# Gathered expert rows on GpSimd: two fetches and two additions per solver period, in front of the first subtraction, instead of one of each behind it

## The chip, the core and the metric

The kernel is one program on one core of a Trainium2 chip. Its five engines run their own instruction streams and meet through semaphores: TensorE (PE) multiplies, VectorE (DVE), ScalarE (ACT) and GpSimd (POOL) work on tiles, and SyncE (SP) issues most of the transfers. The metric is the device time of one execution in microseconds (us).

## The reference, cut to what matters

The reference runs two layers. The first is a delta-rule attention over 8 sequences of 256 tokens with 16 heads of 128, and a mixture of eight experts of which each token gets two. Both add into the same residual rows, so their order is free:

```python
def step(state, inp):
    qt, kt, vt, bt = inp
    pred = jnp.einsum('bhd,bhdv->bhv', kt, state)
    delta = bt[..., None] * (vt - pred)
    state = state + jnp.einsum('bhd,bhv->bhdv', kt, delta)
    ot = jnp.einsum('bhd,bhdv->bhv', qt, state)
    return (state, ot)
...
def expert_body(acc, ws):
    gw, uw, dw, cwe = ws
    y = _mlp(x2d, gw, uw, dw)
    return (acc + cwe[:, None] * y, None)
routed, _ = jax.lax.scan(expert_body, jnp.zeros_like(x2d), (gate_w, up_w, down_w, cw.T))
out = routed.reshape(orig_shape) + _mlp(x, shared_gate_w, shared_up_w, shared_down_w)
```

The second layer is an attention that learns its weights as it goes, and six experts of which each sequence gets two.

## The kernel before

All 2048 tokens stay on the chip, as `X`: 16 tiles (`NT`) of 128 rows by 256 columns. The experts of the first layer run first. They read rows sorted by expert, and write their weighted results, in the same sorted order, to `slot_out` in the chip's memory. Each token has two rows there (`TOP0` is 2), so 32 pieces have to be brought back, one for each of its two experts and each of the 16 tiles. Numbered by `i`, from 0 to 31, a piece is handled in two steps on POOL:

- `fetch(i)` (line 2346) issues one indirect DMA that gathers 128 rows of `slot_out` into buffer `i % GBUF` of `gathered`. From the `GBUF`-th on it first waits until the addition that used the buffer is done.
- `add_fetched(i)` (line 2353) waits for the landing and adds the buffer into a tile of `X`.

Before the first fetch POOL waits until SP's stores of `slot_out` are done (`e_stored`).

The attention of the first layer is a pipeline of 64 units: 16 heads by 4 blocks (`NBLK`) of 512 tokens. `period(h, j)` exists once for each engine, with an order written out by hand, and works on up to five units at a time: `u0` is the newest, `u3` the one whose result is added to `X`. The solver for a unit inverts a triangular matrix in levels and corrects the solution twice. What the engines hand each other near the edited place is this:

- ACT copies the first solution of a unit to `Wu` when PE has made it (`keep_first`, line 1369). POOL's period ends inside the next period of ACT, so the unit is `u1` for POOL and `u2` for ACT here.
- POOL then makes `Rm`, right side minus `Wu` (`rhs_minus(u1, 0, 0)`, lines 2387 to 2393). DVE adds a product of PE to `Rm` and gets `Rb` (`residual`, line 1885), from which PE works out the correction (line 760), which DVE applies (`refine`, line 1891).
- POOL starts the next period with `add_squares` (line 2364): `Osq`, the squared outputs, plus `sqq`, the squared queries. PE waits for it in `sums` (line 814), in the middle of its own fixed order; behind `sums` stand the second product of the correction (line 786), an inversion step (line 746) and the projection of the outputs (line 830).
- POOL's last piece of work ahead of `rhs_minus(u1, 0, 0)` is `gram_rest` (`Gl`, line 2384).

In the first `MERGE` = 9 heads POOL's periods are written out one by one, and behind each of 33 of them (`i` from 0 to 32) stand `fetch(i)` and `add_fetched(i - 1)`. The rest of the heads run in a loop. Nobody but POOL reads `gathered`, and `X` is read again only after the last head.

Of the kernel before, what the change touches and what calls it, by code (L numbers as in the profile page):

```python
# [21 lines left out]
NT = T // P  # L22
BLK = 512
NBLK = T // BLK
# [14 lines left out]
TOP0 = 2  # L39
ROW = D + 16  # L40
TILES0 = TOP0 * T // P + E0 - 1
TG, XBUF, YBUF, GBUF = 3, 3, 2, 3
GROUPS = TILES0 // TG
assert GROUPS * TG == TILES0
SCALE0 = 2.5
# [39 lines left out]
def build(nc, a, out):  # L85
    with ExitStack() as ctx:
# [3 lines left out]
        def sem(name):  # L90
            return ctx.enter_context(nc.semaphore(name))
# [64 lines left out]
        e_stored = [sem(f"e_stored{g}") for g in range(YBUF)]  # L156
# [124 lines left out]
        def units(h, j):  # L281
            return [unit(h, j, back) for back in range(5)]

        def do(step, u, *which):
            if u is not None:
                step(u, *which)
# [2026 lines left out]
        def _(pool):  # L2313
# [32 lines left out]
            def fetch(i):  # L2346
                k, t = divmod(i, NT)
                if i >= GBUF:
                    pool.wait_ge(e_yadd, i - GBUF + 1)
                at = bass.IndirectOffsetOnAxis(ap=slots[:, t, k:k + 1], axis=0)  # L2350
                pool.indirect_dma_start(out=gathered[:, i % GBUF], out_offset=None, in_=slot_out, in_offset=at).then_inc(e_got[i % GBUF], 16)  # L2351

            def add_fetched(i):
                t = i % NT
                pool.wait_ge(e_got[i % GBUF], 16 * (i // GBUF + 1))
                pool.tensor_tensor(X[:, t, :], X[:, t, :], gathered[:, i % GBUF], ALU.add).then_inc(e_yadd, 1)
# [44 lines left out]
                xs = X[:, u.b * TPB + s * NC:u.b * TPB + (s + 1) * NC, :]  # L2401
                pool.tensor_tensor(xs, xs, yrow[:, s], ALU.add).then_inc(pool_x, 1)  # L2402

            def period(h, j):
                u0, u1, u2, u3, u4 = units(h, j)
                do(add_squares, u3)
                do(rhs_minus, u2, 0, 1)
                do(inverse_rms, u3)
                do(add_rows, u3, 0)
                do(add_rows, u3, 1)  # L2410
                do(rhs_minus, u2, 1, 0)
                do(first_rhs, u1)
                do(mask, u2)
                do(rhs_minus, u2, 1, 1)
                do(root, u0)
                do(gram_rest, u1)
                do(rhs_minus, u1, 0, 0)

            pool.wait_ge(a_const, 3 * 16)
            pool.wait_ge(m_added, 2 * NBLK)  # L2420
            MERGE = 9
            for h in range(MERGE):
                for j in range(NBLK):
                    i = h * NBLK + j - 1
                    period(h, j)
                    if i == 0:
                        for n in range(YBUF):
                            pool.wait_ge(e_stored[n], 16 * len(range(n, GROUPS, YBUF)))
                    if 0 <= i < TOP0 * NT:
                        fetch(i)  # L2430
                    if 0 <= i - 1 < TOP0 * NT:
                        add_fetched(i - 1)
            with pool.Fori(0, NH - MERGE) as h:
                for j in range(NBLK):
                    period(h + MERGE, j)
            for j in range(3 - 1):
                period(NH, j)
# [182 lines left out]
```

## Time and profile before

| | us |
|---|---|
| median of 3 executions | 1991.8 |
| lowest and highest of them | 1978.56 and 1995.66 |
| profiled execution, device time | 1994.77 |
| its span, first to last instruction | 1993.0 |
| PE busy | 1793.3 (90%) |
| DVE busy | 1495.4 (75%) |
| ACT busy | 1215.5 (61%) |
| POOL busy | 1071.7 (54%) |

The engines' shares are means over stages with different limits. Up to about 218 us the kernel runs the first layer's routing and experts, up to about 1440 us the 64 units of attention, and then the second layer. A row of a timeline gives start, duration, engine, source line, operation, tiles written and read, and in brackets how long the engine stood idle before it and what released it. The duration of a merged row is that of all its instructions.

### The profile page before, as it was taken

To read this page: it belongs to the slowest core of one execution; us is meant where nothing else is said; L and a number is where in the kernel's file an instruction comes from. 1 tells how busy PE (TensorE), PEld (TensorE's weight loads), DVE (VectorE), ACT (ScalarE), POOL (GpSimd) and SP (SyncE) were. 2 spreads that over 40 slices of the span, in tenths; PEclk is the share of its full clock that TensorE was granted. 3 is DMA by queue.
4 is the path that set the end of the run, shared out by engine and by line. 5 is a ranking of instruction groups with operands and counts; after the bars stand their busy time and mean duration, and the time that the engine had idled before them with its cause. 6 is when DMAs were issued, how large, how long until landed. Compare 5 with 4: busy or idle time off the path is not lost.

```text
span 1993.0 us, 43450 instructions
## 1 busy us (share of the span) xinstructions
PE 1793.3 (90%) x14326; PEld 1321.7 (66%) x14326; DVE 1495.4 (75%) x3475; ACT 1215.5 (61%) x2889; POOL 1071.7 (54%) x1096
## 2 busy tenths in 40 slices
PE   5999899998998998999999999999977778788788
PEld 4577566666666666667777777777755555565566
DVE  5322777787877777788999999999944799779964
ACT  1134566666666666666777777777735577657753
POOL 1600166666656666666666666666652477557731
PEclk8999998998989999899999999999967799989989
DMA  9323010010010000010000000000000000000032
GB/s 307 134 88 107 19 31 30 17 33 18 26 29 21 26 21 29 18 32 21 18 24 26 14 23 26 24 18 21 13 1 1 1 1 2 1 1 1 1 87 74
DMA packets 58670, 69.23 MB, mean 35 GB/s; under 512 B 10608, under 2 KB 47232, under 8 KB 58368
## 3 DMA queue, kind: packets, MB, share of 16 engines
q1 hardware_dynamic: 55511, 59.46, 10.0%
q0 software_dynamic: 3072, 8.65, 1.3%
q8 instruction: 50, 0.82, 0.2%
q14 instruction: 37, 0.30, 0.0%
HBM read 51.00 MB, written 17.10 MB: 34 GB/s over the span
## 4 chain that ended last, share of the span: by engine, by line
PE 60%; DVE 14%; POOL 13%; issue 8%; ACT 4%; DMA 0%; DVEq 0%; SPq 0%; POOLq 0%; ACTq 0%
PE banks L689 9%; PE banks L830 8%; PE banks L814 3%; PE banks L786 3%; PE banks L701 3%; PE banks L709 3%; POOL Rm L2393 2%; PE banks L642 2%; POOL Osq L2364 2%; PE banks L959 2%; POOL Gl L2384 2%; PE banks L661 2%; POOL gathered L2351 2%; PE banks L746 2%; POOL kn L2368 2%
## 5 line engine op out<-in xcount | busy, mean ns | idle before, releaser
L689 PE MATMUL banks<-xnT,hw 128*128 128x512 f32 x768 | 412.7, 621 | 1.7 <-DVE cv L1839 1.7
L1880 DVE CAST_PREDICATED MM<-lmask,banks 128x512 bf16<-128x512 uint32 x384 | 272.7, 710 | 64.0 <-PE banks L754 42.1
L1355 ACT ACTIVATE T<-banks 128x256 bf16<-128x256 f32 x384 | 147.5, 384 | 246.5 <-PE banks L746 234.5
L1839 DVE SCALAR_TENSOR_TENSOR cv<-banks,hc,cv 128x510 f32<-128x510 f32 (+2 forms) x384 | 278.1, 738 | 4.8 <-ACT cv L1305 4.1
L2402 POOL TENSOR_TENSOR X<-X,yrow 128x512 f32<-128x512 f32 x128 | 161.7, 1280 | 123.0 <-ACT yrow L1387 123.0
L830 PE MATMUL banks<-ho,OT 128*128 128x256 f32 x512 | 174.0, 472 | 0.0
L1885 DVE TENSOR_TENSOR Rb<-Rm,banks 128x256 bf16<-128x256 f32 x256 | 106.3, 415 | 73.7 <-PE banks L786 66.3
L2393 POOL TENSOR_TENSOR Rm<-bv,Wu 128x256 f32<-128x256 f32 x64 | 43.1, 673 | 210.6 <-ACT Wu L1369 210.6
L746 PEld LDWEIGHTS banks<-MM,Gb 128*128 128x128 bf16 x1536 | 95.8, 100 | 87.8 <-issue 49.6
L1387 ACT ACTIVATE yrow<-banks,oinv 128x256 f32<-128x256 f32 x256 | 107.5, 471 | 69.6 <-PE banks L830 62.9
L754 PEld LDWEIGHTS banks<-MM,T 128*128 128x128 bf16 x1536 | 107.2, 99 | 59.5 <-issue 38.5
L1839 DVE SCALAR_TENSOR_TENSOR cv<-banks,hcv,cv 128x510 f32<-128x510 f32 (+2 forms) x192 | 141.4, 737 | 0.8 <-ACT cv L1305 0.7
L754 PE MATMUL banks<-MM,T 128*128 128x64 bf16 x1536 | 139.4, 195 | 0.0
L753 PEld LDWEIGHTS banks<-T,MM 128*128 128x128 bf16 x1280 | 99.6, 99 | 51.7 <-ACT T L1355 42.8
L2368 POOL TENSOR_TENSOR kn<-nsum,half_pos 128x4 f32<-128x4 f32 x64 | 65.6, 1025 | 126.4 <-DVE nsum L1851 126.4
L753 PE MATMUL banks<-T,MM 128*128 128x64 bf16 x1280 | 122.1, 196 | 2.6 <-ACT T L1355 2.6
L1309 ACT ACTIVATE raw<-cv 128x512 f32<-128x512 f32 x192 | 121.9, 636 | 1.3 <-DVE cv L1839 1.3
L689 PEld LDWEIGHTS banks<-xnT,hw 128*128 128x128 f32 x768 | 116.3, 190 | 7.5 <-issue 6.3
L2476 POOL TENSOR_TENSOR wT<-wT,XX 128x512 f32<-128x512 f32 x48 | 77.2, 1620 | 81.0 <-DVE XX L2092 81.0
L814 PE MATMUL banks<-ones,Osq 128*128 128x1 f32 x512 | 70.3, 258 | 54.5 <-POOL Osq L2364 54.5
L830 PEld LDWEIGHTS banks<-ho,OT 128*128 128x128 f32 x512 | 108.1, 234 | 11.7
L746 PE MATMUL banks<-MM,Gb 128*128 128x64 bf16 x1536 | 110.5, 196 | 3.8 <-DVE MM L1880 3.6
(322 smaller groups left out, 5025.8 us busy)
## 6 DMA issues: line engine op xcount, KB each, us to landing
MM<-in_eye SPq DMA_DIRECT2D x64, 256.0 KB, 2.6
slot_rows<-zeros SPq DMA_DIRECT2D x1, 5304.0 KB, 20.4
xs<-slot_rows SPq DMA_DIRECT2D x13, 408.0 KB, 3.9
slot_out<-ye SPq DMA_DIRECT2D x13, 384.0 KB, 2.7
hw<-in_hw SPq DMA_DIRECT2D x16, 256.0 KB, 3.3
wgu<-in_wgu SPq DMA_DIRECT2D x1, 2816.0 KB
w1c<-in_ew SPq DMA_DIRECT2D x16, 176.0 KB
X<-in_x SPq DMA_DIRECT2D x4, 512.0 KB, 5.6
```

Of the source, the lines that this page charges most:

```text
L689: ins = pe.matmul(PROJ[t][:], hw[:, kk, t, :], xnT[:, kk, u.b * BLK:(u.b + 1) * BLK], start=(kk == 0), stop=(kk == KD - 1))
L746: last = pe.matmul(o[:, k * 64:(k + 1) * 64], Gb[:, par, k, :], strips(MM[:, u.b, 0, k, :], size, 0, 1), start=True, stop=True)
L753: pe.matmul(o[:, k * 64:(k + 1) * 64], MM[:, u.b, 1, k, :], strips(T1[:, k, :], size, 0, 1), start=True, stop=True)
L754: last = pe.matmul(o[:, (TILES + k) * 64:(TILES + k + 1) * 64], T1[:, k, :], strips(MM[:, u.b, 1, k, :], size, 1, 1), start=True, stop=True)
L814: last = pe.matmul(solve_bank(u)[:, k:k + 1], Osq[:, k, :], ones1[:], start=True, stop=True)
L830: last = pe.matmul(bank[7 - s][:, c * D:(c + 1) * D], OT[:, s * NC + c, :], ho[:], start=True, stop=True)
L1309: act.activation(raw[:, u.b % 2, t, :], cv[:, t, :], ACT.Silu).then_inc(act_silu, 1)
L1355: act.activation(strips(T1[:].rearrange("p i t -> p (i t)"), LEVELS[lv], 0, 1), grams_bank(u)[:, 0:TILES * 64].rearrange("p (k e) -> p k e ...
L1387: last = act.activation(yrow[:, s, c], bank[7 - s][:, c * D:(c + 1) * D], ACT.Copy, scale=oinv[:, u.b % 2, s * NC + c:s * NC + c + 1])
L1839: dve.scalar_tensor_tensor(o, y, taps_of(t)[:, TAPS - 1 - i:TAPS - i], o, ALU.mult, ALU.add).then_inc(dve_conv, 1)
L1880: dve.copy_predicated(dst, m, ps).then_inc(dve_mm, 1)
L2402: pool.tensor_tensor(xs, xs, yrow[:, s], ALU.add).then_inc(pool_x, 1)
```

## The change

`GBUF` goes from 3 to 4, and `MERGE` from 9 to 5. The fetches and additions move into a step `merge(i)` of the period, between `gram_rest` and `rhs_minus(u1, 0, 0)`. It issues `fetch(2 * i)` and `fetch(2 * i + 1)`, and then does `add_fetched(2 * i - 2)` and `add_fetched(2 * i - 1)`. The wait for `e_stored` moves with it. So the 32 fetches stand in 16 periods, and the 32 additions in the 16 periods from the second of these on. `gathered` grows by 1 KB in each partition.

```diff
-TG, XBUF, YBUF, GBUF = 3, 3, 2, 3
+TG, XBUF, YBUF, GBUF = 3, 3, 2, 4
...
-            def period(h, j):
+            def merge(i):
+                if i == 0:
+                    for n in range(YBUF):
+                        pool.wait_ge(e_stored[n], 16 * len(range(n, GROUPS, YBUF)))
+                for n in (2 * i, 2 * i + 1):
+                    if 0 <= n < TOP0 * NT:
+                        fetch(n)
+                for n in (2 * i - 2, 2 * i - 1):
+                    if 0 <= n < TOP0 * NT:
+                        add_fetched(n)
+
+            def period(h, j, i=-1):
...
                 do(root, u0)
                 do(gram_rest, u1)
+                merge(i)
                 do(rhs_minus, u1, 0, 0)
...
-            MERGE = 9
+            MERGE = 5
             for h in range(MERGE):
                 for j in range(NBLK):
-                    i = h * NBLK + j - 1
-                    period(h, j)
-                    if i == 0:
-                        for n in range(YBUF):
-                            pool.wait_ge(e_stored[n], 16 * len(range(n, GROUPS, YBUF)))
-                    if 0 <= i < TOP0 * NT:
-                        fetch(i)
-                    if 0 <= i - 1 < TOP0 * NT:
-                        add_fetched(i - 1)
+                    period(h, j, h * NBLK + j - 1)
```

In program order, POOL before the change, from `root` of one period to `rhs_minus(u2, 0, 1)` of the next, where both a fetch and an addition stand:

```order
L2368 TENSOR_TENSOR kn<-nsum,half_pos 128x4 [waits key_scales]
L2384 TENSOR_TENSOR Gl<-Gk,Gb 128x512 [waits Gb_kept]
L2393 TENSOR_TENSOR Rm<-bv,Wu 128x256 [waits u0_kept]
L2351 DMA gathered<-slot_out,slots 128x256 [waits e_rows_added]
L2356 TENSOR_TENSOR X<-X,gathered 128x256 [waits e_gathered2]
L2364 TENSOR_TENSOR Osq<-Osq,sqq 128x512 [waits q_squared,O_squared]
L2393 TENSOR_TENSOR Rm<-bv,Wd 128x256 [waits u_refined]
```

The fetch and the addition stand between `Rm` and `Osq`. The same place after the change:

```order
L2368 TENSOR_TENSOR kn<-nsum,half_pos 128x4 [waits key_scales]
L2384 TENSOR_TENSOR Gl<-Gk,Gb 128x512 [waits Gb_kept]
L2351 DMA gathered<-slot_out,slots 128x256 [waits e_rows_added] x2
L2356 TENSOR_TENSOR X<-X,gathered 128x256 [waits e_gathered2]
L2356 TENSOR_TENSOR X<-X,gathered 128x256 [waits e_gathered3]
L2393 TENSOR_TENSOR Rm<-bv,Wu 128x256 [waits u0_kept]
L2364 TENSOR_TENSOR Osq<-Osq,sqq 128x512 [waits q_squared,O_squared]
```

Two fetches and two additions now stand between `Gl` and `Rm`, and `Osq` follows `Rm` directly. The orders of PE, DVE, ACT and SP are the same as before.

## Rows read from the trace of the kernel before

**Rows 1.** Busy time by stretch; columns: length, five engines' busy time, PEclk, DMA share, GB/s.
```profile
256.56:934.21 677.65, 625.71 (x5121) 464.22 (x5120) 521.68 (x1281) 427.40 (x1089) 415.97 (x448) 0.92 0.08 25
952.16:1416.40 464.24, 464.24 (x4161) 345.47 (x4160) 422.94 (x1041) 344.43 (x885) 292.38 (x313) 1.00 0.07 22
1393.00:1993.00 600.00, 485.08 (x4034) 365.17 (x4030) 442.65 (x870) 363.69 (x722) 317.47 (x279) 0.90 0.05 15
```

**Rows 2.** Waits, 256.56 to 934.21 us: total, times, longest.
```profile
DVE Rb L1885 <- PE banks L786: 61.2, 32, 2.5
...
PE banks L814 <- POOL Osq L2364: 51.9, 32, 1.7
```

**Rows 3.** POOL's timeline through one period with fetch and addition.
```profile
617.19 0.67 POOL L2393 TENSOR_TENSOR Rm<-bv,Wu 128x256 f32<-128x256 f32 x1 [3.23 <-ACT Wu L1369]
618.04 1.07 POOL L2351 DMA_INDIRECT gathered<-slot_out,slots  x1 [0.17 <-issue]
619.13 0.74 POOL L2356 TENSOR_TENSOR X<-X,gathered 128x256 f32<-128x256 f32 x1
619.82 1.28 POOL L2364 TENSOR_TENSOR Osq<-Osq,sqq 128x512 f32<-128x512 f32 x1
```

**Rows 4.** Busy time of single periods, columns as in rows 1.
```profile
617.19:636.85 19.66, 17.99 (x161) 13.31 (x160) 16.31 (x41) 13.36 (x35) 13.03 (x15) 1.00 0.07 20
...
636.85:659.79 22.94, 21.28 (x161) 15.95 (x160) 16.04 (x41) 13.35 (x35) 13.03 (x15) 0.85 0.06 17
659.79:681.09 21.30, 19.64 (x161) 14.53 (x160) 16.41 (x41) 13.35 (x35) 13.04 (x14) 0.92 0.12 37
681.09:702.55 21.46, 19.79 (x161) 14.62 (x160) 16.39 (x41) 13.35 (x35) 13.02 (x14) 0.92 0.10 25
915.82:934.21 18.39, 18.03 (x161) 13.31 (x160) 16.41 (x41) 13.35 (x35) 11.94 (x14) 1.00 0.12 36
```

**Rows 5.** POOL's timeline through a period with neither.
```profile
969.99 0.67 POOL L2393 TENSOR_TENSOR Rm<-bv,Wu 128x256 f32<-128x256 f32 x1 [3.25 <-ACT Wu L1369]
970.62 1.27 POOL L2364 TENSOR_TENSOR Osq<-Osq,sqq 128x512 f32<-128x512 f32 x1
```

**Rows 6.** POOL's timeline, two scatters of the routing stage, back to back.
```profile
93.02 0.96 POOL L2333 DMA_INDIRECT slot_rows<-xnr,slots  x1 [0.30 <-issue]
94.29 0.96 POOL L2333 DMA_INDIRECT slot_rows<-xnr,slots  x1 [0.30 <-issue]
```

**Rows 7.** POOL's timeline, the last addition, with no fetch before it.
```profile
915.82 0.67 POOL L2393 TENSOR_TENSOR Rm<-bv,Wu 128x256 f32<-128x256 f32 x1 [3.20 <-ACT Wu L1369]
916.45 0.73 POOL L2356 TENSOR_TENSOR X<-X,gathered 128x256 f32<-128x256 f32 x1
917.14 1.28 POOL L2364 TENSOR_TENSOR Osq<-Osq,sqq 128x512 f32<-128x512 f32 x1
```

**Rows 8.** PE's timeline: `sums` behind addition alone, and with neither (from 972.21).
```profile
918.56 0.35 PE L814 MATMUL banks<-ones,Osq 128*128 128x1 f32 x2 [0.36 <-POOL Osq L2364]
...
972.21 0.34 PE L814 MATMUL banks<-ones,Osq 128*128 128x1 f32 x2
```

**Rows 9.** DVE's timeline through the correction, in the period with neither.
```profile
971.22 0.41 DVE L1885 TENSOR_TENSOR Rb<-Rm,banks 128x256 bf16<-128x256 f32 x1
971.55 0.74 DVE L1839 SCALAR_TENSOR_TENSOR cv<-banks,hc,cv 128x506 f32<-128x506 f32 x1
972.41 0.42 DVE L1891 TENSOR_TENSOR Wd<-Wu,banks 128x256 f32<-128x256 bf16 x1
```

**Rows 10.** The fetches as a whole: nanoseconds min/median/max, and landing.
```profile
L2351 POOL DMA_INDIRECT gathered<-slot_out,slots x32: 1057/1067/1072, 240.0 to 893.7; - x32
...
DMA to landing us min/median/max: 2.8/2.9/2.9
```

**Rows 11.** POOL's timeline around the first fetch.
```profile
239.20 0.68 POOL L2393 TENSOR_TENSOR Rm<-bv,Wu 128x256 f32<-128x256 f32 x1 [5.18 <-ACT Wu L1369]
240.04 1.06 POOL L2351 DMA_INDIRECT gathered<-slot_out,slots  x1 [0.17 <-issue]
```

## Prediction

> **What bounds the kernel now.** I read the page first: PE is busy for 90% of the span, and its granted clock is below full in the middle of it. Then I set POOL's timeline against PE's, and cut the attention stage with the view of busy time by stretch. It falls into two parts [rows 1]. From 256.56 to 934.21 us run 32 periods in which POOL has an addition (31 of them with a fetch in front); they take 677.65 us. From 952.16 to 1416.40 us run 26 periods with neither; they take 464.24 us, 17.855 each, with PE busy through all of it and its clock at 1.00. At 17.855 the first 32 would take 571.4. So 106.3 us of the time is there because POOL has these steps where it has them.
>
> The views of waits and of the timeline say how. The fetch and the addition stand between `Rm` and `Osq`, and `Osq` is what PE waits for in `sums`: 51.9 us in 32 waits, 1.66 in most [rows 2, 3]. DVE and ACT wait behind PE, such as DVE at `Rb` for 61.2 us; this is the same stall, seen further on. Two prices can be taken apart [rows 4]. A period with stall whose clock stays at 1.00 takes 19.66, 1.8 more than a plain one: 32 of these are 58. The others, 21.30, 21.46 and 22.94, have the clock at 0.92 or 0.85, so TensorE ran at the lower of its levels (1.2 instead of 2.4 GHz) for a part of them; that is the remaining 48. In the 26 plain periods, where PE does not stall, it never fell.
>
> Ahead of `Rm` POOL stands idle, in both kinds of period, for 3.2 us until ACT has written `Wu` [rows 3, 5]. That idle time costs nothing, and it is where the change puts the work.
>
> **What the change does, part by part.**
>
> Removed: in 32 periods the steps between `Rm` and `Osq`. `Osq` goes back to 0.63 behind the start of `Rm` [rows 5], as in the plain periods. That takes away the whole 106.3, clock included, if PE does not stall otherwise.
>
> Added to 15 periods (`i` from 1 to 15): two fetches and two additions between `Gl` and `Rm`. POOL's hold, from the rows: 0.17 idle ahead of the first fetch and 1.07 for it [rows 3, 10]; two fetches back to back do not occur, and the nearest rows are the scatters, which follow each other with 0.30 between them [rows 6], so 0.30 + 1.07 for the second; 0.02 to the first addition, and 0.69 from start to start of additions and of what follows, twice [rows 3, 7]. Sum: 0.17 + 1.07 + 0.30 + 1.07 + 0.02 + 1.38 = 4.01. The gap holds 3.25 [rows 5]. So `Rm`, and with it `Osq`, starts 0.76 late.
>
> What 0.76 costs is read from the one period of before with an addition and no fetch [rows 7, 8]. There `Osq` started 1.32 behind `Rm` instead of 0.63, 0.69 late; `sums` started 2.74 behind `Rm` (918.56) instead of 2.22 (972.21), 0.52 late, with 0.36 of it an idle PE; the period took 18.39 [rows 4], 0.54 over the mean. So about 0.15 is slack. For 0.76 I take 0.60 a period, and 15 x 0.60 = 9.0.
>
> `Rm` is late here too, which it was not there. DVE took it at 971.22, as soon as it was done at 970.66 and DVE free [rows 5, 9]. At 0.76 later `Rm` is done at 971.42, so `Rb` starts 0.2 to 0.3 late, and the tap behind it ends at 972.5 instead of 972.29. The next correction, at 972.41, slips by 0.1. Its consumer on PE stands behind `sums`, which is 0.6 late already: nothing is added. If it did not lie under that, but had a delay of its own, it could be at most the 0.76 once more.
>
> The other periods: at `i` = 0 two fetches take 2.6 in a gap of 5.2 [rows 11], free. The stores of `slot_out` were done when the fetch of before came, since it started with only the usual 0.17 before it. The new place is some 5 us earlier; if they ended in between, the wait would lie in that same gap. At `i` = 16 two additions take 1.4 in a gap of 3.2, free. Behind `Rm` on POOL stands only what stood there anyway.
>
> Waits: an addition waits for a fetch of the period before. It lands in 2.9 us [rows 10], a period is 18, so it waits for nothing. Fetches `2i` and `2i + 1` need buffers freed by additions up to `2i - 3`, all done in the period before: nothing either. With three buffers the second would wait for an addition that stands behind it, which is what the fourth is for. The loop on POOL starts at the fifth head instead of the ninth. Nearly all of the 26 plain periods lie in that loop and have no idle PE [rows 1], so this costs nothing. Moved bytes are the same; the transfers come in pairs, at a DMA share of 0.08 [rows 1].
>
> **Sum.** -106.3 + 9.0 = -97.3. The profiled execution took 1994.77: 1897.5. It lies 3.0 above the median of the executions shown: 1894.5, so 1895.
>
> Bounds for the 9.0, from below: if the second fetch follows at 0.02 as the addition does, the hold is 3.73 and `Osq` 0.48 late, 0.33 behind the slack: 5 us. Or the slack hides all: 0. From above: both delays in full, 0.54 + 0.76 = 1.3, is 19.5.
>
> **The clock, by rows and by the skill.** In the rows the fall to 1.2 GHz goes with PE's stall of 1.66: it is in three of four such periods and in none of 26 without, and not in the period with a stall of 0.36 [rows 2, 4, 8]. I therefore count the 48 as given back, and expect 1.00 in the new merging periods. The Trainium skill, in TensorE: Matmul & The Clock Gate, section Why this matters for your kernels, warns only of idle gaps that are longer than any of PE's in this stage. By that rule the stall is not what makes the clock fall, and taking it away would not bring the clock back. This case's trace speaks against the rule. The same page, in A second HAM failure mode, says that many small idle spells can make the clock swing too; by that, pauses of half a microsecond could still do it.
>
> **The rivals.**
> - Hidden altogether, 0 to 5 us left: 1886 to 1890. For it: the spacing of 0.30 was measured on scatters. Chance 0.08.
> - Late `Rm` counts on its own, 1.3 a period: 1905. Against it: the consumer stands behind `sums`. Chance 0.08.
> - The clock still falls, once in each of the 15 periods. A period with one such fall cost 21.30 against 19.66, 1.64 [rows 4]: 25 more, 1919. Against it: the 18.39 period kept 1.00. Chance 0.07.
> - The clock falls for a reason other than the stall (that rule above would have it so), and the 48 stay: 1943. Against it: 26 periods at 1.00. Chance 0.03.
> - The change does not do what it says: POOL reaches the gap too late to use it, because its earlier work slips into it, and what is won behind `Rm` is lost ahead of it, so within 1%: some 1990. Against it: `Gl` ends 3.2 ahead of `Rm` in both kinds. Chance 0.02.
> - Slower: two indirect DMAs in a row make POOL wait, for room or for the first to land, and now the solver's subtraction is behind them. The gap and 106.3 / 15 = 7.1 more a period would have to be used up: it decides at a hold of 4.0 + 7.1 = 11 us, and over 1% slower is a hold of 12.5, at 2012 and above. Sixteen scatters in a row at 1.27 apart [rows 6] speak against it. Chance 0.02.
>
> **How the numbers follow.** My forecast has 0.70, at 1895. The executions shown spread from 13 below the median to 4 above; 1895 - 13 = 1882 and, with the case of 1905, 1909 above. Also, the second layer's clock, at 0.90 [rows 1], may fall otherwise when all is earlier by 97 us. The range is 1881 to 1910, which leaves out the clock cases (0.10), the last two (0.04) and some of the spread. Over 1% is about what a measurement of this kernel can tell: faster 0.96, same 0.02, slower 0.02.
>
> **What would show it.** In the profile after: 15 periods of 18.3 to 18.6 us with clock 1.00 between about 256 and 532 us; `Rm` in them with no wait for `Wu`; fetches 1.37 apart; PE's waits for `Osq` 15 of 0.3 to 0.5; plain periods of 17.86 from there on, where the additions stood before. I would be wrong if the pair of fetches holds POOL for clearly more than 2.6, if the clock row stays at 0.92, or if PE waits longer at another step, such as DVE's `Rb`.

## The result and the profile after

The changed kernel takes 1894.81 us, median of 4 executions (1891.9 to 1896.89), against 1991.76 (1978.56 to 1995.66): a ratio of 0.9523, interval 0.9477 to 0.9569. The profiled execution took 1895.93 us with a span of 1894.0. The mean granted clock of TensorE rose from 0.941 to 0.966.

| | before | after |
|---|---|---|
| span, us | 1993.0 | 1894.0 |
| PE busy | 1793.3 | 1741.0 |
| DVE busy | 1495.4 | 1495.5 |
| ACT busy | 1215.5 | 1211.8 |
| POOL busy | 1071.7 | 1069.3 |

DVE, ACT and POOL do the same work. PE's busy time fell by 52 us with the same 14326 matmuls: the matmuls that had run at the lower clock in the merging periods now run at the full one. This is the view of busy time by stretch of the changed kernel. The first row holds the 15 periods with two fetches and two additions, the second the 47 behind them to the end of attention's regular part, the third a single one. Its columns are those of [rows 1].

```profile
257.30:531.38 274.08, 269.35 (x2400) 199.34 (x2399) 245.17 (x601) 199.40 (x510) 217.94 (x240) 1.00 0.12 35
531.38:1370.57 839.19, 832.53 (x7465) 620.70 (x7464) 752.42 (x1851) 614.79 (x1583) 527.59 (x563) 0.99 0.07 21
385.19:403.54 18.35, 18.00 (x162) 13.27 (x161) 16.39 (x42) 13.30 (x35) 14.70 (x17) 1.00 0.16 49
```

The first row answers to the merging stretch of [rows 1]: 274.08 / 15 = 18.27 us a period where it was 677.65 / 32 = 21.18, and a clock of 1.00 where it was 0.92. (The first late `Rm` is the one at which this stretch begins, so that its delay of about 0.7 lies ahead of the row.) The third is one such period, to be laid beside [rows 4]. The next rows are POOL's timeline through the same place as [rows 3], then PE's at `sums`, and two rows of the waits between 257.30 and 531.38 us (total, times, longest).

```profile
381.49 1.07 POOL L2351 DMA_INDIRECT gathered<-slot_out,slots  x1 [0.15 <-issue]
382.86 0.95 POOL L2351 DMA_INDIRECT gathered<-slot_out,slots  x1 [0.30 <-issue]
383.82 1.44 POOL L2356 TENSOR_TENSOR X<-X,gathered 128x256 f32<-128x256 f32 x2
385.19 0.69 POOL L2393 TENSOR_TENSOR Rm<-bv,Wu 128x256 f32<-128x256 f32 x1
385.82 1.29 POOL L2364 TENSOR_TENSOR Osq<-Osq,sqq 128x512 f32<-128x512 f32 x1
```

```profile
387.26 0.24 PE L814 MATMUL banks<-ones,Osq 128*128 128x1 f32 x1 [0.35 <-POOL Osq L2364]
```

```profile
ACT T L1355 <- PE banks L746: 53.1, 60, 2.0
...
PE banks L814 <- POOL Osq L2364: 4.7, 15, 0.4
```

The 3.2 us of idle time ahead of `Rm` are filled, `Rm` starts without any idle time of its own, `Osq` follows 0.63 behind it, and PE's wait for `Osq` fell from 51.9 us in 32 waits [rows 2] to 4.7 in 15. Behind the attention stage nothing moved. The start of the same `Rm`, the 61st, stands at 1416.40 us before and here:

```profile
1317.22 0.68 POOL L2393 TENSOR_TENSOR Rm<-bv,Wu 128x256 f32<-128x256 f32 x1 [3.25 <-ACT Wu L1369]
```

From there to the end are 576.6 us before and 576.8 after. The first `Rm` of all starts at 239.20 before [rows 11] and at 239.26 after. So the whole difference of the two spans lies in the attention stage.

### The profile page after: what moved, and what is told of

Read it like the earlier page. It is cut to its first block, busy times and chain, and to the rows that moved or that the text cites. A ratio compares the mean times of both kernels' runs of the same rounds, so it can differ in the third digit from the quotient of the medians.

```text
span 1894.0 us, 43570 instructions
## 1 busy us (share of the span) xinstructions
PE 1741.0 (92%) x14326; PEld 1282.0 (68%) x14326; DVE 1495.5 (79%) x3475; ACT 1211.8 (64%) x2889; POOL 1069.3 (56%) x1096
## 3 DMA queue, kind: packets, MB, share of 16 engines
q1 hardware_dynamic: 55511, 59.46, 10.6%
## 4 chain that ended last, share of the span: by engine, by line
PE 70%; DVE 13%; POOL 9%; ACT 5%; issue 3%; DMA 0%; DVEq 0%; SPq 0%; ACTq 0%; POOLq 0%
PE banks L689 14%; PE banks L830 6%; PE banks L786 3%; PE banks L814 3%; PE banks L701 3%; PE banks L709 3%; PE banks L805 2%; PE banks L642 2%; PE banks L717 2%; PE banks L760 2%; PE banks L959 2%; PE banks L746 2%; PE banks L754 2%; PE banks L661 2%; PE banks L753 2%
## 5 line engine op out<-in xcount | busy, mean ns | idle before, releaser
L830 PE MATMUL banks<-ho,OT 128*128 128x256 f32 x512 | 143.2, 403 | 0.0
L830 PEld LDWEIGHTS banks<-ho,OT 128*128 128x128 f32 x512 | 89.4, 195 | 7.2
L760 PE MATMUL banks<-Rb,MM 128*128 128x128 bf16 x640 | 89.4, 222 | 4.7 <-DVE Rb L1885 3.9
```

The source lines that it names most:

```text
L760: last = pe.matmul(solve_bank(u)[:, s * P:(s + 1) * P], MM[:, u.b, 1, s * NC + c, :], rhs[:, s, :], start=True, stop=True)
L830: last = pe.matmul(bank[7 - s][:, c * D:(c + 1) * D], OT[:, s * NC + c, :], ho[:], start=True, stop=True)
```

## The experiments

Two questions stayed with a prediction that came out right. Is it the place of the steps, or that half as many periods have them? And are the 48 us that were put down to the clock really a consequence of the stall? A third came up on the way: in two later profiles the changed kernel's attention stage was 5 us slower than in the first, by a wait that the prediction did not have.

The executions are compared with the kernel before on the same chip, whose median was 1991.76, 2001.62, 2001.36, 1989.39 and 1990.99 us in the five measurements. The ratios carry over, the absolute times only roughly. The profile has a finer measure: the time from the first `Rm<-bv,Wu` to the 37th, called the stage here. It is 748.61 us before and 649.34 in the first profile after. These times are differences of starts in POOL's timeline. The last column is the mean over the stretch that is shown or named with each kernel; it begins at the second `Rm<-bv,Wu`. For three and three it gives single periods.

| kernel | median, us | ratio to before (95% interval) | stage, us | a merging period, us |
|---|---|---|---|---|
| before | 1991.8 | 1 | 748.61 | 21.18 |
| changed, first | 1894.8 | 0.9523 (0.9477 to 0.9569) | 649.34 | 18.27 |
| changed, second | 1905.4 | 0.9522 (0.9502 to 0.9542) | 654.29 | 18.60 |
| changed, third | 1904.6 | 0.9580 (0.9542 to 0.9618) | 654.19 | 18.60 |
| one and one in front | 1891.7 | 0.9460 (0.9434 to 0.9485) | 642.46 | 17.86 |
| no fetches, no additions | 1893.0 | 0.9460 (0.9439 to 0.9482) | 643.61 | (17.84) |
| two and two behind | 1991.3 | 0.9957 (0.9928 to 0.9986) | 737.12 | 23.98 |
| one in front, one behind | 1913.2 | 0.9580 (0.9526 to 0.9633) | 660.68 | 18.38 |
| three and three in front | 1927.0 | 0.9654 (0.9596 to 0.9711) | 671.76 | 20.2 to 23.5 |
| before, PE filled, 3 products | 1984.0 | 0.9922 (0.9894 to 0.9949) | 726.46 | 20.40 |
| before, PE filled, 2 products | 1950.7 | 0.9810 (0.9773 to 0.9847) | 702.31 | 19.62 |
| fetches only | 1907.4 | 0.9579 (0.9539 to 0.9618) | 655.89 | 18.61 |
| additions first | 1907.9 | 0.9591 (0.9550 to 0.9633) | 658.44 | 18.87 |
| single fetch, late | 1888.9 | 0.9471 (0.9443 to 0.9500) | 643.86 | 17.86 |

Two and two behind, and the fill with three products, are faster than before by less than 1%; the interval of the fill with two leaves out 1 but reaches to both sides of 2%. All others are faster by over 2%. In five of these profiles (no fetches; one in front, one behind; the fill with two; fetches only; single fetch, late) the clock also fell in the first of the stage's 36 periods, which adds 1.5 to 1.7 us to the stage; in the others it did not. The last column is free of that.

**The changed kernel again.**

> The changed kernel, beside the next two on one chip. Theory (place counts: the steps are hidden in POOL's idle time ahead of Rm, and what does not fit, some 0.46 us in each of 15 periods, is paid as PE's wait for Osq): 1895 us, clock 1.00 in the merging periods, PE waiting for Osq about 5 us in 15 waits. Rival (number counts: what was won is that half as many periods have these steps): the same time here; the next kernel tells them apart.

The ratio is the same. The stage took 654.29 us, 11.8 more than that of one and one in front, and PE waited 10.6 us in 15 waits, but for another thing: for ACT's `T` (line 1355), and not at `sums` for `Osq`. The mechanism expected for the rest was not the one at work here. This is taken up below, as the late wait.

**One fetch and one addition, in front.**

```diff
-                for n in (2 * i, 2 * i + 1):
+                for n in range(1 * i, 1 * i + 1):
...
-                for n in (2 * i - 2, 2 * i - 1):
+                for n in range(1 * i - 1, 1 * i):
...
-            MERGE = 5
+            MERGE = 9
```

(`GBUF` is 3 again.)

> One fetch and one addition in each of 33 periods, as in the kernel before, but ahead of Rm; three buffers, nine heads written out. Theory (place counts): POOL's hold is 0.17 + 1.07 + 0.02 + 0.69 = 1.95 us in a gap of 3.25, nothing is left over: 1888 us, 7 less than the changed kernel, PE not waiting for Osq in these periods. Rival (number of periods counts, each merging period costs its 0.46 whatever it holds): 1888 + 32 x 0.46 = 1903.

This is faster than the changed kernel on the same chip, 1891.7 against 1905.4 us. The difference is 13.7 where 7 was expected; the stages differ by 11.8, for the late wait. Its 32 periods, by stretch:

```profile
262.02:833.53 571.51, 571.50 (x5121) 425.01 (x5120) 520.90 (x1281) 424.00 (x1089) 416.31 (x446) 1.00 0.11 30
```

571.51 / 32 = 17.86, the price of a plain period to a hundredth, with PE busy throughout. The place counts. The number of periods does not: twice as many periods, and nothing is left to pay.

**No merging at all.**

```diff
                 do(gram_rest, u1)
-                merge(i)
                 do(rhs_minus, u1, 0, 0)
```

> Leaves out the 32 fetches and the 32 additions, so the routed experts' rows are never added to X. This is what all the merging costs. Theory: as one_in_front, 1888 us, since hidden work costs nothing; all periods 17.86. Rival (the transfers themselves, or GpSimd's use of memory beside the other engines, cost something even when hidden): lower than one_in_front by more than 2 us.

1893.0 against 1891.7 us: no difference. The stage is 1.2 us longer, by one fall of the clock in its first period (19.04 where the other took 17.36), and the periods behind it are alike:

```profile
266.26:837.25 570.99, 570.98 (x5121) 425.02 (x5120) 520.68 (x1281) 423.17 (x1089) 359.71 (x385) 1.00 0.08 23
```

32 fetches and 32 additions, 58 us of POOL's time, cost nothing when one of each stands in the gap: the rival that the transfers themselves cost something is out, for singles.

**Two and two, put back behind `Rm`.**

```diff
                 do(gram_rest, u1)
-                merge(i)
                 do(rhs_minus, u1, 0, 0)
+                merge(i)
```

> The changed kernel with its pair of fetches and pair of additions put back behind Rm, ahead of Osq; still 16 periods, four buffers. Theory (place counts): Osq is 3.9 us late, 3.75 behind the slack, in 15 periods, 56 us and 1 for the last pair of additions; and the clock falls at each stall, 25 to 50 us: 1888 + 57 + 25 to 50, so 1970 to 1995, hardly faster than before. Rival (pairing is what gained): near 1900 to 1940.

1991.3 against 2001.4 us. Pairing by itself gives half a per cent; the rest of the change's gain is the place. The four buffers and the five heads are in this kernel too, so they are not what gained. PE's waits between 256 and 640 us, and the 15 periods with a full pair:

```profile
PE banks L814 <- POOL Osq L2364: 54.6, 16, 3.6
```

```profile
267.43:627.17 359.74, 306.16 (x2401) 229.25 (x2400) 244.73 (x601) 200.04 (x511) 220.14 (x240) 0.88 0.10 27
```

Longest wait 3.6, expected 3.75; clock 0.88, with a fall in every one of these periods. A period takes 23.98, 6.1 over a plain one: 3.56 is the stall itself and about 2.5 the clock.

**One fetch in front, one addition behind.**

```diff
                 merge(i)
                 do(rhs_minus, u1, 0, 0)
+                if 0 <= i - 1 < TOP0 * NT:
+                    add_fetched(i - 1)
```

(`merge` holds the single fetch alone, with three buffers and nine heads.)

> One fetch ahead of Rm and one addition behind it, in 33 periods. Osq is 0.69 late, as in the one period of before that had an addition alone. Theory: 32 x 0.54 = 17 us over the hidden case, 1905, and the clock stays at 1.00, since PE's idle spells are 0.36. Rival (any stall of PE once a period makes the clock fall): one fall per period at 1.64, 52 more, near 1957.

```profile
PE banks L814 <- POOL Osq L2364: 11.5, 32, 0.4
```

```profile
263.53:851.58 588.05, 576.51 (x5121) 425.88 (x5120) 523.46 (x1281) 426.66 (x1089) 414.56 (x446) 1.00 0.10 29
```

588.05 / 32 is 18.38, 0.52 over a plain period, where 0.54 was read from a single one [rows 4, 7]. PE stalls 0.36 in each of 32 periods, and the clock does not fall in any: one pause of that length in a period does not cost the clock here.

**Three and three, in front.** The additions stand ahead of the fetches, so that three buffers do.

```diff
-                for n in (2 * i, 2 * i + 1):
+                for n in range(3 * i - 3, 3 * i):
                     if 0 <= n < TOP0 * NT:
-                        fetch(n)
+                        add_fetched(n)
-                for n in (2 * i - 2, 2 * i - 1):
+                for n in range(3 * i, 3 * i + 3):
                     if 0 <= n < TOP0 * NT:
-                        add_fetched(n)
+                        fetch(n)
...
-            MERGE = 5
+            MERGE = 4
```

> Three additions and then three fetches ahead of Rm, in 11 and 12 periods, three buffers. POOL's hold is 0.17 + 1.07 + 2 x 1.26 + 3 x 0.69 = 5.8 us in a gap of 3.25: Rm and Osq 2.6 late. Theory (one delay, paid once, at sums or at the correction ahead of it): 9 full periods at 2.45 and one at 1.1, 23 us, and the clock falls at each, 15 to 30 more: 1926 to 1941. Rival (the late Rm counts on its own besides the late Osq): 23 us more than that, 1949 and above.

The delay is paid once: a period takes 20.2, 2.35 over a plain one, where 2.45 was worked out. The rival, a late `Rm` that counts on its own, is out. The clock was missed: it fell three times in the ten periods, in the first two and near the end, and not at each. These are PE's waits from 256 to 560 us, and the first and a later period:

```profile
PE banks L760 <- DVE Rb L1885: 6.1, 9, 1.2
PE banks L814 <- POOL Osq L2364: 5.2, 10, 0.6
PE banks L746 <- DVE MM L1880: 4.2, 9, 1.0
```

```profile
269.57:293.03 23.46, 21.85 (x168) 16.16 (x168) 16.42 (x40) 13.96 (x37) 16.35 (x18) 0.85 0.12 36
371.50:391.70 20.20, 18.30 (x162) 13.24 (x161) 16.19 (x41) 13.33 (x34) 16.27 (x19) 1.00 0.12 34
```

The idle time comes in three pieces, none over 1.2 us, with matmuls between them. The third is a late wait of the kind taken up below: DVE starts line 1880 here 0.6 to 1.4 us behind PE's end in nine of these periods, so the 2.35 need not be the delay of `Rm` alone. Some 1.9 us idle in a period left the clock at 1.00 here; 1.66 in one piece made it fall in three of four periods before.

**The kernel before, with PE's stall filled.** Three products of the identity with 512 columns of `xnT` ahead of `sums`, in the first nine heads. Nobody reads them, since `sums` and what follows overwrite the bank.

```diff
                 pe.wait_ge(act_ot, u.n + 1)
+                if fill:
+                    for k in range(3):
+                        pe.matmul(solve_bank(u)[:], ident[:], xnT[:, 0, 0:BLK], start=True, stop=True)
                 pe.wait_ge(pool_osum, u.n + 1)
```

> The kernel before, with three extra products of the identity with 512 columns of xnT on PE ahead of sums in the first nine heads, into the bank that sums overwrites; their results are not used. They take some 1.65 us at the full clock, about the 1.66 that PE stands idle there. POOL's order is that of before. Theory (the stall makes the clock fall): PE no longer idles, the clock stays at 1.00, and the 48 us of the clock come back although work was added: 1992 - 48 + 3 = 1947, periods of 19.7. Rival (the clock falls for another reason): 1992 or more, and 0.92 in the stage as before.

The clock stayed at 1.00 and the kernel got faster by 17 us, but not by the 45 expected: the products took 2.6 us and not 1.65, longer than the stall they fill, so the periods were 20.40 and not 19.7. With two of them:

> The kernel before with two extra products on PE ahead of sums in the first nine heads, where three made PE's own work 0.7 us longer than the stall (periods of 20.37 at a clock of 1.00). Two take some 1.7, about the stall. Theory (the stall makes the clock fall): clock 1.00 in the stage, periods of 19.65, and 45 us less than the kernel before, near 1955 where that is at 2000. Rival (three products were needed, or the clock falls for another reason): the clock falls in some periods, and the gain is under 25.

```profile
265.35:893.27 627.92, 627.92 (x5249) 446.34 (x5248) 523.43 (x1281) 428.38 (x1089) 415.91 (x447) 1.00 0.10 27
```

Periods of 19.62, as the one in four that kept its clock had before [rows 4], at a clock of 1.00 in all of them; 1950.7 against 1989.4 us. POOL's order is that of before, `Osq` is as late as before, and PE does 1.7 us more work per period. The kernel is 38.7 us faster by the medians (30 to 45 by the interval), for the clock alone. In the stage of the two profiles it is 748.61 - 702.31 = 46.3, and in their spans 1993.0 - 1948.6 = 44.4; what is left to 38.7 is within the spread of the executions. The clock's share of the old stall is then (21.18 - 19.62) x 32 = 50 us, where the prediction had 48. (The 46.3 us are less by the fall in the first period and by one filled period more.) That it fell because PE stood idle is shown, as far as one kernel can.

**The late wait.** In the second and third profile of the changed kernel a merging period took 18.60 and not 18.27. These rows of the third are POOL's two fetches of one period, ACT's row behind them, and PE's wait between 257 and 540 us; the last row is ACT's in the first profile:

```profile
369.83 1.07 POOL L2351 DMA_INDIRECT gathered<-slot_out,slots  x1 [0.17 <-issue]
371.20 0.95 POOL L2351 DMA_INDIRECT gathered<-slot_out,slots  x1 [0.30 <-issue]
```

```profile
372.61 0.38 ACT L1355 ACTIVATE T<-banks 128x256 bf16<-128x256 f32 x1 [1.21 <-PE banks L746]
```

```profile
PE banks L753 <- ACT T L1355: 10.5, 15, 0.9
```

```profile
383.48 0.38 ACT L1355 ACTIVATE T<-banks 128x256 bf16<-128x256 f32 x1 [0.45 <-PE banks L746]
```

ACT waits here for PE's matmuls of line 746. In the first profile, and in plain periods, it is idle for 0.45 and starts within 0.05 of their modelled end. Here it is idle for 1.21 and starts 0.8 later, 1.41 after the second fetch began. In the first profile it started 0.62 after the second fetch began, so the wait ended at the same place against the fetches, and was not late. In the third profile the late wait happens in all 15 periods. After one more measurement of the changed kernel, three kernels were made for it.

> The changed kernel once more, to have it beside the next two on one chip. Its attention stage took 7 us more than the hidden case in the first profile and 12 in the second, where ACT waited for PE at L1355 and went on only 1.4 us after the start of the second fetch. Theory A (overhang: what does not fit the gap is paid once, as PE's wait for Osq, 0.46 a period): 7 over the hidden case. Theory B (beside the overhang, a wait of another engine that ends while POOL issues a fetch ends late, and whether one falls there depends on small shifts): 7 to 12 over it.

The stage was 654.19 us, 11.7 over that of one and one in front, at the upper end of theory B.

Leave out the additions, and count up their semaphore in their place:

```diff
-                pool.tensor_tensor(X[:, t, :], X[:, t, :], gathered[:, i % GBUF], ALU.add).then_inc(e_yadd, 1)
+                pool.sem_inc(e_yadd, 1)
```

> The changed kernel without its additions (the gathered rows are not added to X; the semaphore of the addition is still counted up). POOL's hold is 2.5 us in a gap of 3.25, so Rm and Osq are not late. Theory A: nothing is left, the time of one fetch and one addition in front, 13 under the changed kernel of the same chip. Theory B: the pair of fetches stands where it stood, so the late wait of ACT may stay, up to 0.3 us a period, 0 to 5 us over theory A, with ACT's L1355 idle for 1.2 instead of 0.45.

```profile
377.41 0.95 POOL L2351 DMA_INDIRECT gathered<-slot_out,slots  x1 [0.30 <-issue]
379.59 0.66 POOL L2393 TENSOR_TENSOR Rm<-bv,Wu 128x256 f32<-128x256 f32 x1 [1.24 <-ACT Wu L1369]
```

```profile
378.85 0.38 ACT L1355 ACTIVATE T<-banks 128x256 bf16<-128x256 f32 x1 [1.23 <-PE banks L746]
```

POOL has 1.24 us left over ahead of `Rm`, nothing overhangs, and still the periods take 18.61 and the kernel 1907.4 us, as much as with the additions (1904.6). Theory A, the overhang alone, falls for these two measurements. Nor was theory B right in size: the late wait is not a remainder of 0 to 5 us but all 12. The two fetches hold POOL for 2.49 behind `Gl`, and `Wu` comes 1.24 later, at 3.73 where it was 3.25 [rows 5]. `Rm` would have had to wait for it, and the 3.85 that POOL is held with the additions overhang by only 0.1 to 0.2, about the slack of 0.15.

The pair of additions first, two buffers:

```diff
-                for n in (2 * i, 2 * i + 1):
-                    if 0 <= n < TOP0 * NT:
-                        fetch(n)
                 for n in (2 * i - 2, 2 * i - 1):
                     if 0 <= n < TOP0 * NT:
                         add_fetched(n)
+                for n in (2 * i, 2 * i + 1):
+                    if 0 <= n < TOP0 * NT:
+                        fetch(n)
```

> The pair of additions ahead of the pair of fetches, still ahead of Rm, two buffers. POOL's hold is the same 3.9. Theory A: the time of the changed kernel. Theory B: the fetches now run 1.4 us later, over the waits for the first solution and for T; more of these end late, and the time is 3 to 15 us above the changed kernel's.

1907.9 against 1904.6 us, at the low end of theory B, and not to be told apart by the intervals of the ratios; the stage is 4 us longer. The late wait has moved with the fetches. ACT's is gone, and DVE's for PE's line 754 is now the late one, 1.4 us behind PE's end:

```profile
377.76 0.73 DVE L1880 CAST_PREDICATED MM<-lmask,banks 128x512 bf16<-128x512 uint32 x1 [1.48 <-PE banks L754]
```

Last, one fetch alone where the second of the pair stood, behind an addition and a product of the same shape:

```diff
-                pool.tensor_tensor(X[:, t, :], X[:, t, :], gathered[:, i % GBUF], ALU.add).then_inc(e_yadd, 1)
+                pool.tensor_tensor(X[:, t, :], X[:, t, :], gathered[:, i % GBUF], ALU.add)
+                pool.tensor_tensor(ln_row[:, 0, 0, :], X[:, 15 - t, :], X[:, 15 - t, :], ALU.mult).then_inc(e_yadd, 1)
```

(The fetch stands behind these two in `merge`, in the version with one of each, with three buffers and nine heads.)

> One addition, one product of the same shape whose result is not used, and then one fetch, all ahead of Rm, in 33 periods. POOL's hold is 2.7 us in a gap of 3.25, so nothing overhangs. The single fetch starts where the second fetch of the changed kernel's pair starts, 1.5 us behind the end of Gl. Theory B1 (a fetch at that place, in front of ACT's wait for PE at L1355, makes that wait end late, with no need of a pair): 32 periods of 18.4 to 18.8, some 25 us over the kernel with one fetch and one addition in front, ACT idle for 1.2 at L1355. Theory B2 (it takes the pair, back to back): periods of 17.9 and its time, ACT idle there for 0.45.

```profile
397.49 1.07 POOL L2351 DMA_INDIRECT gathered<-slot_out,slots  x1 [0.16 <-POOL ln_row L2357]
```

```profile
398.26 0.39 ACT L1355 ACTIVATE T<-banks 128x256 bf16<-128x256 f32 x1 [0.45 <-PE banks L746]
```

Periods of 17.86, ACT idle for 0.45, a ratio of 0.9471: the same as one and one in front. A single fetch at that place delays nothing; it took a pair, back to back. What in a pair holds another engine's wait back is open, and so is why the first profile of the changed kernel did not have it.

## Why the prediction was right, point by point

- **Time.** 1895 was forecast, 1894.81 measured, in the range of 1881 to 1910.
- **What is removed: 106.3 us.** Right. The stage lost 748.61 - 649.34 = 99.3; with the 6.9 left over (next point) that is 106.2.
- **What is left: 15 x 0.60 = 9.0 us.** A little too large. The stage of the first profile is 649.34 - 642.46 = 6.9 us over that of one and one in front, 0.46 a period. POOL's hold was put at 4.01; the second fetch takes 0.95 and not 1.07, which makes it 3.9. Taken off the gap of 3.25 and less the slack of 0.15, that is 0.5 a period: the way of reckoning was right, and one of its terms too large. PE's stall is 0.31 a period (4.7 in 15), where the row from which the price was taken had 0.36 [rows 8]. In the later profiles the same term was 11.8 us, inside its bounds of 0 and 19.5, but by the late wait, which none of the bounds was built on. The step "behind `Rm` on POOL stands only what stood there anyway" was right for POOL, and left out what a pair of fetches does to ACT.
- **Where `Rm` is late, and the once-only delay.** Right: three and three in front cost 2.35 a period where one delay gives 2.45 and two would give twice that.
- **The clock.** Right for this change, and now shown by filling the stall. The share, 48 us, measured as 50. The rule of the Trainium skill weighed against it, in TensorE: Matmul & The Clock Gate, section Why this matters for your kernels, warns only of idle gaps longer than the 1.66 us here, and the runs contradict it: the case of 1943 did not come, and the fill removed every fall in the 32 periods while POOL's lateness stayed. The other passage of the Trainium skill, on the same page, in A second HAM failure mode, that many small idle spells can make the clock swing, was not borne out at 0.36 us once a period in 32 periods. What comes nearer to it is the stage's first period: PE idles there in pieces of up to 0.9 us, after others of up to 1.1 in the 15 us before, and the clock fell in five of 14 profiles.
- **The zero-cost items.** The moved wait for `e_stored` cost nothing: the first fetch started at 234.24 us, at once behind `Gl`, in a gap of which 2.70 was left. The additions waited for no landing, the loop on POOL that starts earlier has periods of 17.8 to 18.0 as before.
- **The rivals.** "Slower" needed a hold of 11 us; it was 3.9. "Does not do what it says" is out by POOL's rows.
- **Luck.** The agreement to 0.2 us is partly chance: the second and third measurement gave 1905 us on chips where before took 2002 and 1989, and the ratio of the third, 0.9580, would have meant 1908 here.

The version with one fetch and one addition in front and three buffers beats both kernels, with a ratio of 0.946 to before. It is also the smaller edit: only the place is changed.

## What to carry to other kernels

Before work of an in-order engine is spread thinner or batched, look for the idle time that the engine has in each period, and put the work ahead of the step that the idle time waits for, in pieces that fit. Price a stall at its own length and at what the clock does behind it: here the stall cost 1.8 us a period and the clock another 1.6. And a wait that goes away should be looked for again in a second profile: the overhang that one profile showed was not what cost the time in the next.

## What the runs showed of the hardware

- Idle PE in a period of attention, and the granted clock: 0.36 us never made it fall (32 periods); 1.66 us did in three of four periods; 3.56 us in each of 15; about 1.9 us in three pieces in three of ten; four or five pieces of up to 0.9 us, in the stage's first period, in five of 14 profiles. With the 1.66 filled by useless products, the clock stayed at 1.00 for 32 periods, and the kernel, with more work, was 2% faster (0.9810, 0.9773 to 0.9847).
- POOL is held for 1.07 us by an indirect DMA that gathers 128 rows of 1 KB, and for 0.95 by one that follows directly, with 0.30 between them. A pair takes 2.32.
- With two or three such DMAs back to back, single waits of ACT or DVE for PE that would have ended in that time ended mostly 0.5 to 1.4 us behind PE's end: in every merging period where the pair stands in front, and in 11 of 15, at the low end of that, where it stands behind `Rm` (DVE's line 1891, 0.54 to 0.62). With a single one they ended at most 0.33 behind it, and with no fetch near at most 0.26. The one first profile of the changed kernel is an exception that nothing here explains.
